# An eight-layer graph and feed-forward network on one core: order of the last expert stage, halves in the top-k search, single tiles in a norm, an earlier bias load

## The chip, the cores and the metric

One core of a Trainium2 chip runs the whole program, one launch from the inputs in HBM to the output in HBM. The metric is the device time of that launch in microseconds, the median of several runs.

## What is computed

Eight layers work one after another on 1250 rows (nodes, or tokens) of 512 numbers, each adding its result to the rows: a graph convolution, a mixture of experts, two graph attention layers with a dense expert layer between them, a feed-forward layer with weights merged from task vectors, a neighbour mean with a layer norm, and a last mixture of experts. Cut to the layers that the change touches:

```python
# L2_gnn: attention, h = x @ W1, then masked softmax over the neighbours, with bias b1, later b2
# L2_ffn: W1m, W2m merged from 8 task vectors
h   = relu(x @ W1m.T + b1m)
out = h @ W2m.T + b2m
y   = layernorm(x + out) * lng + lnb
# L3_ffn: NUM_EXPERTS = 32, GROUP_SIZE = 4, D_FF = 1365, k = 1250 // 32 = 39
Sm = softmax(x @ W_router + b_router)
G, idx = top_k(Sm.T, 39)                        # each expert takes its 39 best tokens
up  = einsum('gjkh,ghf->gjkf', x[idx], W_up)    # one up matrix for each group of 4 experts
act = silu(up + b_up)
E   = einsum('ekf,efh->ekh', act, W_down) + b_down   # one down matrix for each expert
y   = zeros.at[idx].add(G[..., None] * E)
```

## The kernel before, in words

All data are float32. Rows are held as ten tiles of 125 rows by 512. Each layer is a stage (`Stage`) with its own buffers, and at its end all engines meet at a barrier. Inside a stage every engine has its own program, written out by hand, and engines wait for each other by semaphores only; the order of the calls in `sp_program`, `pe_program`, `act_program`, `dve_program` and `pool_program` is the order of the work. SP issues the plain loads and stores in one queue, in order, and GpSimd (POOL) issues indirect gathers and scatters, and some plain copies.

**`gnn2`, the attention stage.** At its start `sp_program` (L2004) issues the mask, the weights, then the two bias vectors (L2008) and further loads. TensorE turns the ten normed tiles, waits for the biases, turns them (L2194), waits until VectorE has copied them (L2362), and then makes the attention rows (`pe_rows`, L2086). ScalarE copies these rows (L2279), and a store and loads through HBM spread them for VectorE's masked maxima (`dve_max`), which need the mask, while TensorE makes the linear products (`pe_linear`, L2114), which need the weights.

**`ffn2`, the merged stage.** At its end TensorE adds up ten tiles of the result in eight PSUM banks. VectorE works by groups of 4, 4 and 2 tiles: `dve_group` takes statistics of each tile (L2575), then mean and variance, and the reciprocal of the root that ScalarE takes; ScalarE normalises each tile out of PSUM (L2524); `dve_finish` multiplies by the merged gain (L2589), adds to the rows (L2591) and takes the statistics for the next layer (L122, `tile_statistics`). The next group's statistics stand ahead of a group's finish.

**`last_layers`, the last two layers.** First products, neighbour sums and the layer norm, tile by tile (`dve_tile`, L2791 on), with router logits. Then `Router.dve_softmax`, and `dve_slots` with `pe_slots` choose the tokens: TensorE turns the ten tiles of weights into 32 rows of 1250, VectorE copies them out of PSUM (L733) and five times finds the eight largest (MAX8, L737), their places (FIND_INDEX8, L738) and blanks them (MATCH_REPLACE8, L741; four times). That makes 40 slots, of which the last has its weight set to 0. The lists are turned and copied to `sw` and `si` (L749, L750).

Then eight groups of four experts. Per group i: POOL gathers 4 x 40 token rows (`pool_gather`), TensorE turns them (`pe_tokens`), VectorE copies them to `xgT` (`dve_tokens`), TensorE makes the up products of all four experts in 11 parts of the inner dimension (`pe_up`, 88 matmul records), ScalarE applies SiLU into the one buffer `hT` (L2929), TensorE makes the down products in two pairs of experts (`pe_down`, 44 records a pair), VectorE multiplies by the weights (`dve_rows`, L2987), and POOL scatters with addition to the output (`pool_scatter`, L2846), each scatter waiting for the one before it. The program order on TensorE is up(i), tokens(i+1), down(i) with both pairs. Up matrices (2.8 MB each) have two buffers, down matrices (2.8 MB each) a ring of five. `sp_program` loads into a buffer as soon as its last reader is done: up matrix i+2 waits for the end of up(i), down matrix e for the pair that used e-5. The last two down matrices are loaded in three parts each, in turn.

## Time and profile before

| | |
|---|---|
| median of 3 runs | 2931.55 us (2931.22 to 2933.32) |
| profiled execution, its own time | 2929.89 us |
| its span in the trace | 2928.1 us |
| mean granted TensorE clock | 0.908 of full |
| busy: TensorE, VectorE, ScalarE, GpSimd | 84%, 55%, 29%, 20% of the span |
| stage `gnn2` begins, `ffn2` begins | 1528, 2253 us |
| `last_layers` begins, tokens chosen, span ends | 2377, 2592, 2928 us |

Times of rows are microseconds from the start of the span. PE is TensorE's matmul side, PEld its weight loads, DVE is VectorE, ACT ScalarE, POOL GpSimd, and SPq the issuing of DMAs by SP. L2846 is a line of the kernel. A granted clock of 1.00 is TensorE at 2.4 GHz, 0.50 at 1.2 GHz. A DMA share of 1 means that all 16 DMA engines are busy.

### The profile page before, as it was taken

The numbers are of one execution on the slowest core, as the hardware profiler recorded it, in microseconds if no ns is written. First come the engines' busy times: TensorE is split into PE (matmuls) and PEld (weight loads), VectorE is DVE, ScalarE is ACT, GpSimd is POOL, SyncE is SP. The second block draws the span as 40 slices with busy tenths as digits, with TensorE's granted clock in tenths as the row PEclk, the third lists the DMA queues.
The fourth block names the chain that finished last, engine by engine and source line by source line (L and its number), as shares of the span: only waits on it lengthen the run. The fifth ranks groups of instructions, "written<-read, shape, count | busy, mean of one in ns | idle before, by whom it ended". The sixth has DMA issues, their size and how long they took to land. (4 is left out here: it accounts for less than half of the span.)

```text
span 2928.1 us, 31276 instructions
## 1 busy us (share of the span) xinstructions
PE 2461.4 (84%) x10766; PEld 1562.6 (53%) x10766; DVE 1624.7 (55%) x3768; ACT 837.2 (29%) x1860; POOL 585.8 (20%) x563
## 2 busy tenths in 40 slices
PE   3899947999957999985568899999999869958877
PEld 1355446999944777774443455344554434434443
DVE  9999353132424889986246898627963354431100
ACT  0155011111112776771111465105641110101110
POOL 0000065455303555420110000000000101012211
PEclk9899957999977999996789999999999989979988
DMA  4000363776724555543443553214541331459996
GB/s 135 0 1 27 120 187 100 260 230 217 260 73 131 155 156 155 152 88 128 125 137 121 194 193 106 89 62 138 189 132 54 127 138 46 144 195 337 347 347 222
DMA packets 195434, 440.43 MB, mean 150 GB/s; under 512 B 25179, under 2 KB 45387, under 8 KB 194798
## 3 DMA queue, kind: packets, MB, share of 16 engines
q1 hardware_dynamic: 156958, 344.67, 35.1%
q0 software_dynamic: 38320, 93.76, 12.3%
q8 instruction: 88, 1.44, 0.2%
q14 instruction: 68, 0.56, 0.1%
HBM read 394.21 MB, written 43.93 MB: 150 GB/s over the span
## 5 line engine op out<-in xcount | busy, mean ns | idle before, releaser
L2124 PE MATMUL psum<-x_res,HH 125*128 125x512 f32 (+1 forms) x960 | 351.7, 525 | 20.2 <-DVE x_res L2314 20.2
L2124 PEld LDWEIGHTS psum<-x_res,HH 125*128 125x128 f32 x960 | 181.3, 193 | 179.8 <-issue 156.4
L1101 POOL DMA_INDIRECT recd<-edge_records,edge_slots x160 | 193.1, 1207 | 293.8 <-issue 287.2
L1468 POOL DMA_INDIRECT hg<-HT,srcidx x196 | 191.2, 975 | 258.5 <-PE psum L1589 128.6
L1630 ACT ACTIVATE hg<-hg,ex 128x129 f32<-128x129 f32 x784 | 235.2, 389 | 1.6
L1589 PE MATMUL psum<-hg,Dh 128*125 128x258 f32 x784 | 208.0, 424 | 6.8 <-DVE ACC L1531 4.3
L2114 PE MATMUL psum<-W,XO 128*125 128x512 f32 x480 | 209.0, 596 | 0.0
L2891 PE MATMUL psum<-wd,XN 128*40 128x512 f32 (+1 forms) x550 | 162.3, 621 | 31.6 <-DMA wd<-in_L_ffn_b_down 22.2
L1589 PEld LDWEIGHTS psum<-hg,Dh 128*125 128x125 f32 x784 | 160.1, 209 | 40.7 <-issue 6.8
L1135 PE MATMUL psum<-xgT,w 128*128 128x187 f32 x1024 | 172.8, 329 | 4.1 <-DMA w<-in_L_ffn_w 4.1
L1135 PEld LDWEIGHTS psum<-xgT,w 128*128 128x128 f32 x1024 | 166.2, 194 | 8.7 <-DMA w<-in_L_ffn_w 5.8
L1144 PE MATMUL psum<-sums_room,w 128*128 128x187 f32 x1024 | 166.1, 322 | 0.0
L1144 PEld LDWEIGHTS psum<-sums_room,w 128*128 128x128 f32 x1024 | 162.9, 190 | 0.0
L2307 DVE SCALAR_TENSOR_TENSOR x_res<-rows,ASD,x_res 125x1250 f32<-125x1250 f32 x80 | 120.7, 1511 | 71.8 <-ACT x_res L2228 71.8
L2114 PEld LDWEIGHTS psum<-W,XO 128*125 128x125 f32 x480 | 90.1, 189 | 115.0 <-issue 114.9
L1208 ACT ACTIVATE sums_room<-psum,b1T 128x187 f32<-128x187 f32 x128 | 53.3, 417 | 282.6 <-PE psum L1135 282.5
L2228 ACT ACTIVATE x_res<-rows,AS 125x1250 f32<-125x1250 f32 x80 | 106.5, 1334 | 95.6 <-PE psum L2124 93.8
L2987 DVE TENSOR_SCALAR x_res<-psum,slot_w 40x512 f32<-40x512 f32 x32 | 23.9, 747 | 195.2 <-PE psum L2891 194.7
L1499 DVE CUSTOM_DVE_ANT_0 junk<-mb,psum 125x512 f32<-125x512 bf16 x196 | 123.1, 684 | 7.8 <-issue 0.9
L2294 DVE CUSTOM_DVE_ANT_0 junk<-MK,rows 125x1250 bf16<-125x1250 bf16 x80 | 116.9, 1461 | 16.4 <-DMA rows<-ROWS 12.4
L2314 DVE SCALAR_TENSOR_TENSOR x_res<-x_res,MK 125x1250 f32<-125x1250 f32 x80 | 116.3, 1454 | 5.4 <-DMA MK<-CT 4.6
L389 PE MATMUL psum<-Sh,Dh 128*125 128x512 bf16 (+1 forms) x588 | 116.4, 347 | 1.8 <-ACT H L596 0.7
(520 smaller groups left out, 3977.0 us busy)
## 6 DMA issues: line engine op xcount, KB each, us to landing
w<-in_L_ffn_w SPq DMA_DIRECT2D x64, 1024.0 KB, 15.1
wd<-in_L_ffn_W_down SPq DMA_DIRECT2D x24, 2560.0 KB
MK<-CT SPq DMA_DIRECT2D x80, 625.0 KB, 3.8
wu<-in_L_ffn_W_up SPq DMA_DIRECT2D x8, 2730.0 KB, 16.4
wd_ahead<-in_L_ffn_W_down SPq DMA_DIRECT2D x6, 2560.0 KB
rows<-ROWS POOLq DMA_DIRECT2D x24, 625.0 KB, 7.2
w<-in_L_ffn_W SPq DMA_DIRECT2D x18, 512.0 KB
t<-in_L_ffn_tv_W SPq DMA_DIRECT2D x16, 512.0 KB
```

The costliest lines, as they stand in the source:

```text
L1101: pool.indirect_dma_start(out=g.recd, out_offset=bass.IndirectOffsetOnAxis(ap=g.posi[:, c:c + 1], axis=0), in_=g.E8[:, c, :], in_offset=No ...
L1135: ins = pe.matmul(g.PS[:, m, 0:CAP], W1[k][:, c, m * 128:(m + 1) * 128], xgT[e % 2][:, c, 0:CAP], start=(c == 0), stop=(c == KC - 1))
L1144: ins = pe.matmul(g.PS[:, 4 + 2 * (e % 2) + c // 2, (c % 2) * SL:(c % 2) * SL + CAP], W2[k][:, m, c * 128:(c + 1) * 128], hT[k % 2][:, m, ...
L1468: pool.indirect_dma_start(out=hg[j % RING][:, c, :], out_offset=None, in_=g.HT, in_offset=bass.IndirectOffsetOnAxis(ap=g.srcidx[:, j * CH ...
L1499: dve.tensor_tensor_reduce(junk[:, h, :], mb[:], bank(h), 1.0, NEG, ALU.add, ALU.max, qm[:, h:h + 1]).then_inc(*top.up())
L1589: ins = pe.matmul(bank(6 + w)[:, 0:HW // 2], Dh[j % 3][:, c, :], hg[j % RING][:, c, w * (HW // 2):(w + 1) * (HW // 2)], start=(c == 0), st ...
L1630: ins = act.activation(heads[:, h, :], heads[:, h, :], ACT.Copy, scale=ex[j % 2][:, c, h:h + 1])
L2114: ins = pe.matmul(PS[0:TP, 2 + i % 3, :], XO[:, c, t * TP:(t + 1) * TP], Wt[:, c, w * 512:(w + 1) * 512], start=(c == 0), stop=(c == kc(l) ...
L2124: return pe.matmul(flat[:, at:at + x1 - x0], HH[:, k, h * DH + c * 128:h * DH + c * 128 + 128], z[n % 4][:, x0:x1], start=(k == 0 and i < ...
L2294: dve.tensor_tensor_reduce(junk[:], MK[0:TP, t, :], RR[h][0:TP, :], 1.0, NEG, ALU.add, ALU.max, MX[:, h, t:t + 1]).then_inc(*head_max.up())
L2307: dve.scalar_tensor_tensor(z[n % 4], RR[2 * (h % 2)][0:TP, :], ASD[:, k, h:h + 1], z[n % 4], ALU.add, ALU.max).then_inc(*mx.up())
L2891: ins = pe.matmul(g.PS[place[k], 4 + k, :], hT[0:deep[m], m, k * SL:(k + 1) * SL], WDn[ring(GS * i + k)][0:deep[m], m, :], start=(m == 0), ...
```

## The change

Four edits.

1. **Last expert stage.** TensorE's order becomes: up(0), tokens(1), and then for each group down pair 0, up(i+1), tokens(i+2), down pair 1. `hT` is held twice, so ScalarE may write group i+1's while group i's is read. SP's order: after the first pair of down loads of a group stands the up load i+3, which waits for up(i+1). The second-to-last down matrix is issued before the wait for the last pair's buffer. POOL gathers three groups ahead and puts a gather between the scatters of a group. 39 token rows in place of 40.
2. **Shorter search.** The turned weights lie as 64 rows of 625 (two halves of the tokens for each expert). Five rounds find 40 of each half; the second half's list is reversed in its first 39 places, and both lists are merged with one comparison by place: the larger of v0[j] and v1[38-j].
3. **Single tiles.** In `ffn2` groups are gone: VectorE handles a tile from its statistics to its sum, ScalarE takes only the root.
4. **Early biases.** In `gnn2` the bias loads stand first in SP's queue.

The diff, cut to its core:

```diff
     def slots(self, count, keep, WT=None, choice=None):
+        self.at = [2 * (t % (NT // 2)) + t // (NT // 2) for t in range(NT)]
+        self.WT = WT if WT is not None else s.sb("weights_by_expert", [2 * ne, N // 2])[:]
...
     def pe_slots(self):
-        for t in range(NT):
-            ins = pe.transpose(g.PS[0:ne, t // 4, (t % 4) * TP:(t % 4 + 1) * TP], self.L[:, t, :],
-                               g.ident[0:TP, 0:TP])
+        for j in range(NT // 2):
+            ins = pe.transpose(g.PS[0:2 * ne, j // 4, (j % 4) * TP:(j % 4 + 1) * TP],
+                               self.L[:, 2 * j:2 * j + 2, :].rearrange("p a e -> p (a e)"), g.ident[0:TP, 0:TP])
...
+        for k, (first, second) in enumerate(((self.val, self.rval), (self.idf, self.rid))):
+            pe.transpose(g.PS[0:self.count, k, 0:ne], first[0:ne, :], g.ident[0:ne, 0:ne])
+            ins = pe.transpose(g.PS[0:self.count, 2 + k, 0:ne], second[ne:2 * ne, :],
+                               g.ident[ne:2 * ne, ne:2 * ne])
...
     def dve_slots(self):
+        dve.tensor_copy(WT[:, 0:4 * TP], g.PS[0:2 * ne, 0, 0:4 * TP]).then_inc(*v.up())
+        dve.tensor_copy(WT[:, 4 * TP:5 * TP], g.PS[0:2 * ne, 1, 0:TP]).then_inc(*v.up())
...
+        dve.tensor_copy(self.rval[ne:2 * ne, 0:n], val[ne:2 * ne, n - 1::-1]).then_inc(*v.up())
+        dve.tensor_copy(self.rval[ne:2 * ne, n:], val[ne:2 * ne, n:]).then_inc(*v.up())
         step(dve.tensor_copy(idf[:], ix[:]))
-        step(dve.tensor_scalar(val[:], val[:], 0.0, None, ALU.max))
-        if self.kept < self.count:
-            step(dve.memset(val[:, self.kept:self.count], 0.0))
+        dve.tensor_scalar(self.rid[ne:2 * ne, 0:n], idf[ne:2 * ne, n - 1::-1], float(N // 2), None,
+                          ALU.add).then_inc(*v.up())
+        dve.tensor_scalar(self.rid[ne:2 * ne, n:], idf[ne:2 * ne, n:], float(N // 2), None, ALU.add).then_inc(*v.up())
...
+        dve.tensor_copy(self.sw[:], v1).then_inc(*v.up())
+        step(dve.tensor_copy(self.diff, t1))
+        dve.tensor_tensor(self.ge, v0, self.sw[:], ALU.is_ge).then_inc(*v.up())
+        step(dve.tensor_tensor(self.diff, t0, self.diff, ALU.subtract))
+        dve.tensor_tensor(self.sw[:], v0, self.sw[:], ALU.max).then_inc(*v.up())
+        step(dve.tensor_tensor(self.diff, self.diff, self.ge, ALU.mult))
+        dve.tensor_tensor(self.si[:], t1, self.diff, ALU.add).then_inc(*v.up())
...
         def sp_program():
+            for l, b in enumerate((b1, b2)):
+                sp.dma_start(br[l * C8:(l + 1) * C8, :], b.rearrange("(c p) -> c p", p=128)).then_inc(*b_in.up(16))
             sp_mask(0)
             sp.dma_start(Wt[:, 0:KC, :], rows_of(W1)).then_inc(*w_in.up(16))
-            for l, b in enumerate((b1, b2)):
-                sp.dma_start(br[l * C8:(l + 1) * C8, :], b.rearrange("(c p) -> c p", p=128)).then_inc(*b_in.up(16))
...
+        def dve_tile(t):
             step = Chain(dve, v)
+            one, res = slice(t, t + 1), g.PS[0:TP, t % 8, :]
+            dve.wait_ge(*down.at(t + 1))
+            step(dve.bn_stats(st[:, t, :], res))
+            step(dve.bn_aggr(mv[:, t, :], st[:, t, :]))
+            dve.tensor_scalar(rs[:, one], mv[:, t, 1:2], EPS, None, ALU.add).then_inc(*var.up())
+            dve.scalar_tensor_tensor(XN[0:TP, t, :], res, mv[:, t, 0:1], lng[:], ALU.subtract,
+                                     ALU.mult).then_inc(*normed.up())
+            dve.wait_ge(*root.at(t + 1))
+            dve.reciprocal(rs[:, one], rs[:, one]).then_inc(*ready.up())
+            dve.wait_ge(*normed.now())
+            dve.wait_ge(*ready.now())
+            step(dve.scalar_tensor_tensor(g.X[:, t, :], XN[0:TP, t, :], rs[:, one], g.X[:, t, :], ALU.mult, ALU.add))
+            tile_statistics(g, t)
...
-    SG = GS * SL
+    SG = GS * K
...
             sp_down(NR - 2, 0, FM, lw[ring(NR - 2)])
+            sp.wait_ge(*mu.at(FM))
+            sp_up(2)
             for i in range(NG - 1):
-                if i + 2 < NG:
-                    sp.wait_ge(*mu.at(FM * (i + 1)))
-                    sp_up(i + 2)
                 for e in range(GS * i + NR, GS * i + NR + GS):
                     if e < NE:
                         sp.wait_ge(*md.at((e - NR) // 2 + 1))
                     if e < NE - 2:
                         sp_down(e, 0, FM, lw[ring(e)])
+                    elif e == NE - 2:
+                        for j, (m0, m1) in enumerate(PARTS):
+                            sp_down(e, m0, m1, last_pair[j])
+                    if e == GS * i + NR + 1 and i + 3 < NG:
+                        sp.wait_ge(*mu.at(FM * (i + 2)))
+                        sp_up(i + 3)
             for j, (m0, m1) in enumerate(PARTS):
-                for e in (NE - 2, NE - 1):
-                    sp_down(e, m0, m1, last_pair[j])
+                sp_down(NE - 1, m0, m1, last_pair[j])
...
             for i in range(NG):
-                if i + 2 < NG:
-                    pool_gather(i + 2)
                 for k in range(GS):
+                    if k == GS // 2 and i + 3 < NG:
+                        pool_gather(i + 3)
                     pool_scatter(GS * i + k)
...
             pe_tokens(0)
+            pe_up(0)
+            pe_tokens(1)
             for i in range(NG):
-                pe_up(i)
+                pe_down(i, 0)
                 if i + 1 < NG:
-                    pe_tokens(i + 1)
-                pe_down(i)
+                    pe_up(i + 1)
+                if i + 2 < NG:
+                    pe_tokens(i + 2)
+                pe_down(i, 1)
...
             for i in range(NG):
-                if i:
-                    act.wait_ge(*md.at(GS // 2 * i))
+                if i >= 2:
+                    act.wait_ge(*md.at(GS // 2 * (i - 1)))
...
             for i in range(NG):
-                if i == 0:
-                    dve_tokens(0)
-                if i + 1 < NG:
-                    dve_tokens(i + 1)
-                dve_rows(i)
+                dve_rows(i, 0)
+                if i + 2 < NG:
+                    dve_tokens(i + 2)
+                dve_rows(i, 1)
```

## Rows read from the trace of the kernel before

**Rows 1.** Stretches, last stage: us; busy of each engine; PEclk, DMA share, GB/s.

```profile
2585.00:2616.00 31.00, 16.21 (x106) 15.66 (x106) 7.18 (x13) 5.52 (x12) 7.52 (x8) 0.67 0.08 22
...
2650.00:2700.00 50.00, 42.18 (x241) 21.15 (x239) 6.13 (x8) 4.33 (x11) 16.23 (x14) 0.97 1.05 334
...
2902.00:2928.00 26.00, 12.83 (x60) 3.42 (x56) 2.99 (x4) 0.00 (x0) 5.72 (x4) 0.83 0.12 17
```

**Rows 2.** Timeline, TensorE: start, us, instruction, idle before and its releaser.

```profile
2831.14 11.05 PE L2891 MATMUL psum<-wd,XN 128*40 128x512 f32 x44 [7.45 <-DMA wd<-in_L_ffn_b_down]
```

**Rows 3.** Timeline of SP's queue, last stage.

```profile
2615.68 0.39 SPq L2691 DMA_DIRECT2D wu<-in_L_ffn_W_up  x1
2626.99 0.39 SPq L2695 DMA_DIRECT2D wd_ahead<-in_L_ffn_W_down  x1
```

**Rows 4.** Chain of waits, near its end: start, us, what.

```profile
2872.02 11.10 PE psum L2891 x44
2883.11 12.16 PE psum L2869 x88
...
2895.74 19.11 PE psum L2891 x88
```

**Rows 5.** Timeline of POOL, last stage, the scatters.

```profile
2884.19 1.43 POOL L2846 DMA_INDIRECT out<-x_res,slot_i  x1 [8.62 <-DVE x_res L2987]
2892.57 1.43 POOL L2846 DMA_INDIRECT out<-x_res,slot_i  x1 [6.94 <-DMA out<-x_res,slot_i]
...
2915.92 1.43 POOL L2846 DMA_INDIRECT out<-x_res,slot_i  x1 [3.47 <-DVE x_res L2987]
2920.29 1.43 POOL L2846 DMA_INDIRECT out<-x_res,slot_i  x1 [2.94 <-DMA out<-x_res,slot_i]
```

**Rows 6.** Timeline, TensorE, start of the attention stage.

```profile
1546.32 0.28 PE L2194 MATMUL psum<-ident,bias_rows 16*128 16x16 f32 x1 [7.03 <-DMA bias_rows<-in_L_gnn_b]
1546.87 10.41 PE L2086 MATMUL psum<-XO,att 128*8 128x512 f32 x24 [0.27 <-DVE biases L2362]
```

**Rows 7.** Stretches at the start of the attention stage, columns as rows 1.

```profile
1537.00:1541.00 4.00, 2.11 (x15) 1.32 (x13) 1.19 (x3) 2.49 (x5) 0.00 (x0) 1.00 1.04 410
...
1545.00:1550.00 5.00, 3.42 (x5) 0.68 (x6) 0.17 (x1) 0.00 (x0) 0.00 (x0) 0.50 1.03 388
```

**Rows 8.** POOL's plain stores of normed tiles (tensor XND), issue to landing.

```profile
DMA to landing us min/median/max: 2.7/2.7/8.6
```

**Rows 9.** Timeline, VectorE, end of the merged stage.

```profile
2333.99 0.70 DVE L2575 BATCH_NORM_STATS2 st<-psum 125x6 f32<-125x512 f32 x1 [5.59 <-PE psum L2500]
2336.50 0.70 DVE L2575 BATCH_NORM_STATS2 st<-psum 125x6 f32<-125x512 f32 x1 [1.80 <-PE psum L2500]
...
2362.05 1.28 DVE L2575 BATCH_NORM_STATS2 st<-psum 125x6 f32<-125x512 f32 x2
...
2376.03 0.69 DVE L122 BATCH_NORM_STATS2 ln_st<-x_res 125x6 f32<-125x512 f32 x1
```

**Rows 10.** Timeline, VectorE, one tile of `last_layers`' `dve_tile`: both statistics.

```profile
2543.55 0.69 DVE L2798 BATCH_NORM_STATS2 st<-wd 125x6 f32<-125x512 f32 x1
...
2546.33 0.69 DVE L2809 BATCH_NORM_STATS2 ln_st<-x_res 125x6 f32<-125x512 f32 x1
```

**Rows 11.** Groups by form, VectorE, search: count, busy us, mean ns, idle before.

```profile
L737 DVE MAX8 slot_value<-records 32x8 f32<-32x1250 f32 x5 | 7.3, 1451 | 0.2
L738 DVE FIND_INDEX8 top_index<-slot_value,records 32x8 uint32<-32x1250 f32 x5 | 7.2, 1442 | 0.0
L741 DVE MATCH_REPLACE8 records<-slot_value,records 32x1250 f32<-32x1250 f32 x4 | 5.7, 1432 | 0.0
L733 DVE COPY records<-psum 32x500 f32<-32x500 f32 x2 | 1.3, 662 | 2.4 <-PE psum L716 2.4
L733 DVE COPY records<-psum 32x250 f32<-32x250 f32 x1 | 0.4, 397 | 0.0
```

**Rows 12.** Timeline, VectorE, a small operation behind the search.

```profile
2590.62 0.17 DVE L742 CAST slot_token<-top_index 32x40 f32<-32x40 uint32 x1
```

More of the change, by code:

```diff
@@ L645, in __init__ @@
         self.v = s.sig("dve_steps")
+        self.at = list(range(NT))
         self.loaded, self.out = s.sig("router_loaded"), s.sig("logits_out")
@@ L2415, in ffn2 @@
         norm = Norm(g, s, XT=XT, XN=XN)
-        groups = ((0, 4), (4, 8), (8, NT))
         def sp_program():
@@ L2518, in act_program @@
                                    bias=b1c[:, f:f + 1]).then_inc(*relu.up())
-            for i, (t0, t1) in enumerate(groups):
-                act.wait_ge(*var.at(i + 1))
-                act.activation(rs[:, t0:t1], rs[:, t0:t1], ACT.Sqrt).then_inc(*root.up())
-                act.wait_ge(*ready.at(i + 1))
-                for t in range(t0, t1):
-                    act.activation(XN[0:TP, t, :], g.PS[0:TP, t % 8, :], ACT.Identity, bias=nb[:, t:t + 1],
-                                   scale=rs[:, t:t + 1]).then_inc(*normed.up())
+            for t in range(NT):
+                act.wait_ge(*var.at(t + 1))
+                act.activation(rs[:, t:t + 1], rs[:, t:t + 1], ACT.Sqrt).then_inc(*root.up())
         def pool_program():
@@ L2601, in dve_program @@
             dve.wait_ge(*lnb_in.at(1))
-            dve_group(0, *groups[0])
-            for i in range(len(groups)):
-                if i + 1 < len(groups):
-                    dve_group(i + 1, *groups[i + 1])
-                dve_finish(i, *groups[i])
+            for t in range(NT):
+                dve_tile(t)
         sp_program()
@@ L2657, in last_layers @@
         first = Norm(g, s, xn=[XN[:, u, :] for u in range(2)], xT=xT[0])
-        place = [slice(64 * (k % 2), 64 * (k % 2) + SL) for k in range(GS)]
+        place = [slice(64 * (k % 2), 64 * (k % 2) + K) for k in range(GS)]
         free = WU[1][:].rearrange("p a b -> p (a b)")[:, NT * D:]
@@ L2667, in last_layers @@
                            view(spare, TP, nw, NT, NE)))
-        rt.slots(SL, K, old[0:NE, 0:N])
+        rt.slots(SL, K, old[0:2 * NE, 0:N // 2], [g.iota_tp[0:SL, k * NE:(k + 1) * NE] for k in range(2)])
         norm = rt.norm
-        xg, xgT = XN[0:SL, 0:GS, :], view(XN_all[:, 2 * GS:, :].rearrange("p a d -> p (a d)"), 128, 0, KC, SG)
-        hT = XN_all[:, GS:2 * GS, :].rearrange("p a d -> p (a d)")[:, 0:FM * SG].rearrange("p (m n) -> p m n", m=FM)
-        wo = g.X[0:SL, 0:2 * GS, :]
+        xg, end = XN[0:K, 0:GS, :], XN_all[:, 2 * GS:, :].rearrange("p a d -> p (a d)")
+        xgT = view(end, 128, 0, KC, SG)
+        half = view(XN_all[:, GS:2 * GS, :].rearrange("p a d -> p (a d)"), 128, 0, FM, SG)
+        hT = [[half[:, m, :] for m in range(FM)], [old[:, m * SG:(m + 1) * SG] for m in range(FM - 1)] +
+              [end[:, KC * SG:(KC + 1) * SG]]]
+        wo = g.X[0:K, 0:2 * GS, :]
         listed, gathered = s.sig("slots_listed"), s.sig("gathered0")
@@ L2978, in dve_tokens, with dve_rows @@
                             g.PS[:, 0:2, 0:2 * SG]).then_inc(*tc.up())
-        def dve_rows(i):
-            for k in range(GS):
+        def dve_rows(i, pair):
+            for k in (2 * pair, 2 * pair + 1):
                 e = GS * i + k
                 row = wo[:, e % (2 * GS), :]
-                dve.wait_ge(*md.at(GS // 2 * i + k // 2 + 1))
+                dve.wait_ge(*md.at(GS // 2 * i + pair + 1))
                 if e >= 2 * GS:
                     dve.wait_ge(*scattered.at(16 * (e - 2 * GS + 1)))
-                dve.tensor_scalar(row, g.PS[place[k], 4 + k, :], rt.sw[:, 0, e:e + 1], None,
+                dve.tensor_scalar(row, g.PS[place[k], 4 + k, :], rt.sw[0:K, e:e + 1], None,
                                   ALU.mult).then_inc(*ev.up())
```

115 lines of the change are left out of this document (43 added, 72 removed).

## The prediction

> **What bounds the kernel now.** The profile was read in this order: busy time over stretches of the last stage, the chain of waits, the timeline of each queue, and then the two places further up that the change touches. The kernel runs its stages one behind the other with a barrier between, so microseconds saved in one stage are saved at the end, if nothing in that stage takes them back.
>
> In the last stage the reader is to see two regimes [rows 1]. From 2585 to 2616 the DMA engines stand almost still (share 0.08, 22 GB/s): tokens are chosen, gathered and multiplied by the first up matrix, and no further weights may be loaded until that product frees its buffer. From 2650 on the share is 1.05, and after 2902 it is 0.12. TensorE waits for down weights there, 7.45 us before one pair [rows 2]. So from about 2616 to 2902 this stage is a fixed amount of bytes at a fixed rate. Reordering TensorE can't shorten it. What counts is when the stream may start, whether it ever runs dry, and what is left once it has ended. The start is the load of the third up matrix at 2615.68, which waits for the end of the first up products; the next load waits for the first down pair at 2626.99 [rows 3]. The rest is the chain at the end: a pair of downs at 2872.02 as soon as its weights land, up products 12.16, both last pairs 19.11 [rows 4], then the scatters, of which each waits for the one before [rows 5].
>
> **Early biases (attention stage).** The bias rows are issued behind the mask and the weights, and TensorE takes them only at 1546.32 after 7.03 us without work; the attention products follow at 1546.87 and take 10.41 [rows 6]. Two small transfers at the head of the queue should land well before the transposes ahead of them in TensorE's order end, at 1546.32 - 7.03 = 1539.3. Then the products start 1546.87 - 1539.9 = 6.9 earlier. There is more: the granted clock was 1.00 (2.4 GHz) from 1537 to 1541, behind the transposes, and 0.50 (1.2 GHz) from 1545 to 1550, behind the idle time [rows 7]. The products ran at half speed until a little after 1550, about 3.5 us, half of which, 1.8, goes too: together 8.7. Against it: the products' row is then stored while the DMA engines are still full (share 1.03 until 1550 [rows 7]). Stores on this queue landed in 2.7 us when quiet, at most 8.6 [rows 8]. I take 1 us of that, as the engines empty within a microsecond or two of that store: **-7.7**, bounds -5.8 and -8.8. Mask and weights move back by under 1 us and are used later than 1551, which costs nothing. VectorE's chain and TensorE's product chain of the stage both begin behind this point, so the gain stays.
>
> **Single tiles (merged stage).** Before, VectorE starts its first statistics at 2333.99 and starts its last at 2376.03, ending at 2376.72 [rows 9]; TensorE delivers a tile each 2.5 to 2.6 us, and VectorE waits for whole groups, then works them off. The new tile is the sequence which the last stage already has: from its first statistics to the second 2.78 us [rows 10], plus 0.6 until the next may start (two statistics in a row take 1.28, one 0.70 [rows 9]) = 3.38. Ten make 33.8, more than TensorE's 26, so VectorE alone decides: 2333.99 + 33.8 + 0.1 = 2367.9, **-8.8**. The 2.78 hold ScalarE's root already. Bounds -8.2 (0.05 more on each tile) and -9.0.
> The Trainium skill ("VectorE: DVE Perf Modes", section on the TRN2 errata) says that each VectorE instruction pays a fixed latency, that many small tiles pay it per tile, and that one should tile to 512 elements or more, which speaks against this edit; by its fixed term of some 150 cycles, thirty tiny operations in place of nineteen cost 1.7 us more, which would leave 7.1 if they were not in the 2.78 already.
>
> **Shorter search.** Five rounds on 1250 elements: five times 1451, five times 1442, four times 1432 ns [rows 11]. The copies there take 662 ns for 500 elements and 397 for 250: 1.06 ns per element, so 625 fewer save 0.66 on each of 14 instructions, 9.3. No row shows 64 partitions for 32, but row lengths, not partitions, set the price everywhere here. Five transposes for ten save 1.1 of their 2.3; copying 625 columns for 1250 saves 0.7. Added: two more small operations ahead of the last transposes, two more transposes, and seven for two operations behind them, in four dependent steps; small ones cost 0.17 [rows 12]. That is 0.3 + 0.15 + 0.87. Copies with a reversed order are in no row: at best they cost like the others, at worst 0.3 more each. Net 9.3 + 1.1 + 0.7 - 1.3 = **-9.8**, bounds -9.0 and -10.3. This shifts the gathers, the first up products and the restart of the stream one for one; weights for the first groups land before 2585 [rows 1].
>
> **Order of the last stage.** Loads, their bytes and their wait for the first up products stay. 39 columns for 40 save at most a fortieth of 12.16, 0.3, of the first up products; taken as nothing. The stream must not dry up: the fourth up matrix now waits for the second up products, at 2626.99 + 12.2 = 2639.2, while two down matrices (33 matrices in the 286 us from 2616 to 2902: 8.7 each) are under way until 2644.4; the next two down matrices wait for the second pair, 1.7 + 9.6 later, 2650.5, while the up matrix runs until 2653. It holds, by 2 to 3 us. So the stream ends as before, less the shift. The down matrix after the wait in [rows 4] and its three followers keep their places; two places earlier (8.2 us each, from 2831.14 to 2872.02 for five [rows 2, 4]) its predecessor lands at 2855.6. TensorE: first pair of the seventh group 2855.6 + 10.6 (between 9.6 and the 11.1 after a wait) = 2866.2, last up products +12.2 = 2878.4, then three pairs of 9.6 and 0.6 of waiting: 2907.8 instead of 2914.85, **-7.0 on TensorE**. But scatters take 8.4 us each under load (2884.19 to 2892.57) and 4.4 when quiet [rows 5]. Experts 26 and 27 are ready at 2888.8 (before: 2884): 2889.8, 2898.2, 2904.7, 2909.1, 2913.5, the last at 2917.9 instead of 2920.29. The chain of scatters, not TensorE, sets the end. That is -2.4; as 8.4 is one interval and they may be quicker, I take **-2.8**, with 0 and -7.4 as bounds.
> A scatter now has 39 rows for 40. By the Trainium skill ("DMA: Bandwidth & Descriptors", section "Why a DMA increments its semaphore by 16 and not by 1") a transfer is spread over the largest number of engines up to 16 that divides its rows, 10 for 40 and 13 for 39; if that held for these, the loaded scatters would be a quarter shorter and the term nearer -5.
>
> **Sum.** 7.7 + 8.8 + 9.8 + 2.8 = 29.1. The profiled execution took 2929.9 (span 2928.1), so 2900.8; the median of the runs is 2931.55, 1.7 above it, and the forecast stands on that: **2902.5**. All least gains, with 1 us of a dry stream, give 22 less; all largest 36.5 less: 2909.6 and 2895.1.
>
> **Rivals.**
> (a) The tail follows TensorE. For it: the scatters of the pairs before may be quicker than 8.4. Then the last term is 7: 2898.3. Chance 0.18.
> (b) The biases gain nothing: another load or store takes their place, or VectorE's masks decide. Against it: both chains of the stage start behind these products. 2910.2. Chance 0.07.
> (c) The stream runs dry, and the kernel is slower. SP's queue is in order: the up load that waits for the next group's up products holds back the two down loads behind it. If the matrices under way were used up in that time, each of five or six groups would stand idle for up to 12.2 us of up products; with 5 groups 61 us: 2963.5. It decides as soon as the loads queued ahead last less than the 22 us of a pair and the up products; in steady flow six loads, some 50 us, stand ahead, so only the start (2 to 3 us of margin) is near. Chance 0.03.
> (d) The search is not shortened: the doubled partitions cost double. 2912.3. Chance 0.04.
> The forecast has 0.64, and 0.04 is left for what I overlook. A measurement can tell 0.2% here, 5.9 us. All but (c) are faster by more; half of the rest goes to faster and half to no change: 0.95 faster, 0.02 same, 0.03 slower. The range, 2895 to 2911, holds the forecast's bounds, (a) and (b).
>
> **What would show it.** Right: TensorE doesn't idle ahead of the bias transpose; the merged stage ends some 34 us after its first statistics; eight-element searches near 0.79 us; the third up matrix loaded 26.3 us earlier than now; share 1.05 without a dip until about 2876; the last scatters 4.4 apart without waiting for VectorE. Wrong: a dip of the DMA share in the first 40 us of the stream, pairs of 39 rows that scatter slower, or a search that keeps its 21 us.

## Result and the profile after

The changed kernel takes **2893.56 us** (median of 4 runs, 2890.28 to 2897.89) against 2932.44 for the kernel before beside it: ratio 0.9872, 95% interval 0.9859 to 0.9886, so 38.9 us less. The forecast was 2902.5 us with a range of 2895 to 2911; the sign is right, and the gain was 1.4 us larger than even the range allowed. The profiled execution took 2891.68 us, its span is 2889.7 us at a mean granted clock of 0.916.

Stretches of the last stage in the changed kernel (us; busy of PE, PEld, DVE, ACT, POOL; PEclk, DMA share, GB/s):

```profile
2555.00:2585.00 30.00, 15.04 (x104) 14.77 (x105) 7.71 (x24) 5.00 (x11) 7.41 (x8) 0.66 0.38 134
2616.00:2666.00 50.00, 49.43 (x285) 25.51 (x282) 6.78 (x9) 5.45 (x14) 12.28 (x10) 1.00 1.05 350
2867.00:2889.00 22.00, 8.57 (x40) 2.73 (x36) 1.50 (x2) 0.00 (x0) 5.61 (x4) 0.78 0.14 21
```

They answer to [rows 1]: the same three regimes, but from 30 to 80 us into the stream it carries 350 GB/s, where from 34 to 84 us it had 334 before, at the same share of 1.05. These windows flatter the change: over the whole stream it is 343 GB/s against 338. TensorE's clock is 1.00 in this stretch (0.97 before).

SP's queue, as [rows 3]:

```profile
2585.75 0.39 SPq L2686 DMA_DIRECT2D wu<-in_L_ffn_W_up  x1
2597.06 0.39 SPq L2690 DMA_DIRECT2D wd_ahead<-in_L_ffn_W_down  x1
...
2608.91 0.39 SPq L2686 DMA_DIRECT2D wu<-in_L_ffn_W_up  x1
```

The third up load starts at 2585.75 instead of 2615.68, the next down load 11.3 us later as before, and the fourth up load now 23.2 us behind the third instead of 37.4.

The chain of waits at the end, as [rows 4] (start, us, what):

```profile
2844.76 9.78 DMA wd<-in_L_ffn_b_down
2854.53 0.14 issue
2854.67 9.66 PE psum L2889 x44
...
2865.12 0.76 DVE x_res L2991
2865.89 0.04 issue
2865.92 9.66 PE psum L2889 x44
...
2877.80 3.39 DMA out<-x_res,slot_i
```

and POOL's last scatters, as [rows 5]:

```profile
2855.08 1.41 POOL L2845 DMA_INDIRECT out<-x_res,slot_i  x1 [12.92 <-DVE x_res L2991]
2863.03 1.40 POOL L2845 DMA_INDIRECT out<-x_res,slot_i  x1 [6.54 <-DMA out<-x_res,slot_i]
2869.54 1.41 POOL L2845 DMA_INDIRECT out<-x_res,slot_i  x1 [5.11 <-DMA out<-x_res,slot_i]
2873.69 1.40 POOL L2845 DMA_INDIRECT out<-x_res,slot_i  x1 [2.74 <-DMA out<-x_res,slot_i]
2877.80 1.41 POOL L2845 DMA_INDIRECT out<-x_res,slot_i  x1 [2.71 <-DVE x_res L2991]
2881.98 1.40 POOL L2845 DMA_INDIRECT out<-x_res,slot_i  x1 [2.78 <-DMA out<-x_res,slot_i]
```

with VectorE's rows of the last pair:

```profile
2875.61 1.53 DVE L2991 TENSOR_SCALAR x_res<-psum,slot_w 39x512 f32<-39x512 f32 x2 [9.73 <-PE psum L2889]
```

Of the last six scatters the profile gives four to the landing of the one before, and those of 2855.08 and 2877.80 to VectorE. The second of these is doubtful. The first of VectorE's two rows was done after half of 1.53 us, at 2876.4, and before the change the scatter followed 1.04 us behind such a start (2914.88 to 2915.92), which would have been 2876.65 here. It came 4.11 us behind the scatter before it, like its neighbours (4.15 and 4.18), so it too waited for a landing. No up products stand there any more: the last two pairs are separate, with 1.6 us between them for VectorE.

Attention stage, as [rows 6]:

```profile
1537.57 0.23 PE L2202 MATMUL psum<-ident,bias_rows 16*128 16x16 f32 x1
1538.41 8.56 PE L2094 MATMUL psum<-XO,att 128*8 128x512 f32 x24 [0.61 <-ACT XO L201]
```

The same two stretches of that stage as [rows 7]:

```profile
1537.00:1541.00 4.00, 3.39 (x14) 1.25 (x14) 0.17 (x1) 1.16 (x2) 0.00 (x0) 1.00 1.04 412
1545.00:1550.00 5.00, 3.71 (x18) 1.83 (x17) 0.41 (x2) 1.20 (x1) 0.58 (x1) 1.00 0.99 366
```

TensorE has no idle time ahead of the bias rows, the clock stays at 1.00 (2.4 GHz), and the products take 8.56 us instead of 10.41, 1.85 less.

Merged stage, VectorE, two successive tiles, as [rows 9]:

```profile
2326.95 0.68 DVE L2578 BATCH_NORM_STATS2 st<-psum 125x6 f32<-125x512 f32 x1
...
2329.66 0.69 DVE L122 BATCH_NORM_STATS2 ln_st<-x_res 125x6 f32<-125x512 f32 x1
2330.27 0.68 DVE L2578 BATCH_NORM_STATS2 st<-psum 125x6 f32<-125x512 f32 x1
```

A tile takes 3.32 us. The search, groups by form (count, busy us, mean ns), as [rows 11]:

```profile
L737 DVE MAX8 half_value<-records 64x8 f32<-64x625 f32 x5 | 4.0, 804 | 0.2
L738 DVE FIND_INDEX8 top_index<-half_value,records 64x8 uint32<-64x625 f32 x5 | 4.0, 795 | 0.0
L741 DVE MATCH_REPLACE8 records<-half_value,records 64x625 f32<-64x625 f32 x4 | 3.1, 786 | 0.0
...
L742 DVE COPY turned_value<-half_value 32x39 f32<-32x39 f32 x1 | 0.2, 173 | 0.0
```

An instruction on 64 rows of 625 takes 647 ns less than one on 32 rows of 1250, close to the 663 that 625 elements cost at the 1.06 ns of the copies in [rows 11]; the doubled partitions add nothing that can be seen. The copy in reversed order (L742) takes 173 ns, a straight operation of that size 0.17 us [rows 12].

**Where the 38 us are.** The stretches below are cut at issues of SP's queue (the attention stage's first load, its first load of counts, the merged stage's first load, the last stage's first and third up load) and at the end of the weight stream, which is where the DMA share falls for good. That end is read in windows of 2 us, so the last two rows are good to about 1 us.

| us in the profiled runs | before | after | difference | forecast |
|---|---|---|---|---|
| up to the attention stage | 1528.5 | 1527.1 | -1.4 | 0 |
| attention stage to its counts (biases) | 101.3 | 94.5 | -6.8 | -7.7 |
| from there to the merged stage (same code) | 623.4 | 620.4 | -3.0 | 0 |
| merged stage to first up load (tiles) | 143.8 | 135.4 | -8.4 | -8.8 |
| first to third up load (search) | 218.7 | 208.4 | -10.3 | -9.8 |
| weight stream | 285.7 | 280.9 | -4.8 | 0 |
| tail behind the stream | 26.7 | 23.0 | -3.7 | -2.8 |

Three upstream terms came as forecast (25.5 against 26.3). What was missed is the weight stream, 4.8 us shorter, and 4.4 us in stretches that run the same code in both kernels.

### The profile page after: what moved, and what is told of

It is laid out like the page before. It is cut to its first block and busy times, and to the rows that moved or that the text cites. A ratio compares the mean times of both kernels' runs of the same rounds, so it can differ in the third digit from the quotient of the medians.

```text
span 2889.7 us, 31294 instructions
## 1 busy us (share of the span) xinstructions
PE 2447.9 (85%) x10763; PEld 1555.9 (54%) x10763; DVE 1617.5 (56%) x3786; ACT 831.9 (29%) x1857; POOL 587.2 (20%) x563
## 5 line engine op out<-in xcount | busy, mean ns | idle before, releaser
L1109 POOL DMA_INDIRECT recd<-edge_records,edge_slots x160 | 194.5, 1216 | 292.4 <-issue 285.7
L2991 DVE TENSOR_SCALAR x_res<-psum,slot_w 39x512 f32<-39x512 f32 x32 | 23.9, 747 | 187.8 <-PE psum L2889 187.3
L2302 DVE CUSTOM_DVE_ANT_0 junk<-MK,rows 125x1250 bf16<-125x1250 bf16 x80 | 116.9, 1461 | 17.9 <-DMA rows<-ROWS 13.8
L2268 ACT ACTIVATE x_res<-x_res 125x1250 f32<-125x1250 f32 x80 | 99.0, 1237 | 30.6 <-DVE x_res L2315 29.6
```

Source lines behind the costliest of these rows:

```text
L1109: pool.indirect_dma_start(out=g.recd, out_offset=bass.IndirectOffsetOnAxis(ap=g.posi[:, c:c + 1], axis=0), in_=g.E8[:, c, :], in_offset=No ...
L2302: dve.tensor_tensor_reduce(junk[:], MK[0:TP, t, :], RR[h][0:TP, :], 1.0, NEG, ALU.add, ALU.max, MX[:, h, t:t + 1]).then_inc(*head_max.up())
```

## Experiments

Each group of four ran on one chip, beside the kernel before, whose median was 2961.0 us for t1 to t4, 2964.6 for t5 to t8, 2931.2 for t9 to t12 and 2935.0 (one run) for t13 to t16. Medians are compared within a group only. Stretches of the trace are compared over all. "Stream" is the time from the third up load to the end of the weight stream; in the five traces with the old order and 40 rows its length was 284.9 to 285.7.

**t1: the changed kernel again**, with no edit.

> The changed kernel once more, as the yardstick of the next three. Measured before: 2893.6 us, and from the load of the third up matrix to the end of the weight stream 280.3 us, against 286.3 in the kernel before; the prediction had taken this as unchanged. If that was chance of one profiled execution (drift), this one's stream lies anywhere between 280 and 286. If it belongs to the change, it is 280 +- 1 again, and the time 2893.6 +- 2.

Measured 2924.4 us, ratio 0.9887 (0.9870 to 0.9904), 36.6 us less than before. Stream 281.3, third up load to the end of the span 304.4 (first trace 304.0; before 312.4). The shorter stream belongs to the change. Drift is ruled out for it: the six traces of the new order with all transfers and with the last two matrices loaded as in the change (the first one, t1, t3, t7, t9, t10) have 280 to 281.6.

**t2: old order, 39 rows.** On all queues the order of before, for instance on TensorE:

```diff
-            pe_up(0)
-            pe_tokens(1)
             for i in range(NG):
-                pe_down(i, 0)
+                pe_up(i)
                 if i + 1 < NG:
-                    pe_up(i + 1)
-                if i + 2 < NG:
-                    pe_tokens(i + 2)
-                pe_down(i, 1)
+                    pe_tokens(i + 1)
+                for pair in range(GS // 2):
+                    pe_down(i, pair)
```

> The changed kernel with the old order of the last stage on all queues (both down pairs together, up load i+2 ahead of the down loads, two gathers ahead, the last two matrices interleaved), but 39 rows. Theory 'rows' (39 rows for 40 in gathers and scatters shorten the stream): stream 280, only the tail's 2.4 us are lost, 2896. Theory 'order' (the new order keeps the stream fuller): stream 286, tail 26, 2902. Theory 'drift': stream anywhere, 2896.

**t3: new order, 40 rows**, the same in places, transposes, weights and scatters; the last parts of the second `hT` lie elsewhere to make room.

```diff
-    SG = GS * K
+    SG = GS * SL
...
-        xg, end = XN[0:K, 0:GS, :], XN_all[:, 2 * GS:, :].rearrange("p a d -> p (a d)")
+        xg, end = XN[0:SL, 0:GS, :], XN_all[:, 2 * GS:, :].rearrange("p a d -> p (a d)")
```

> The changed kernel with its new order but 40 rows an expert in gathers, products and scatters (the 40th keeps the weight that the merge gives it, so each expert adds one token more than the reference). Theory 'rows': stream 286, 2893.6 + 6 + 0.3 for the first up products = 2900. Theory 'order': stream 280, 2894. Theory 'drift': 2894, stream anywhere.

**t4: both undone** (the edits of t2 and t3).

> Both undone: old order and 40 rows in the last stage, with the shorter search, the single tiles and the early biases kept (the 40th row keeps its weight here too). Stream 286 and tail 26 by 'rows' and by 'order': 2902. 'Drift': 2896. Beside the kernel before (2932.4) this is what the three upstream edits are worth: 26.3 by the prediction, so 2905 to 2906 if nothing else was gained there; 29 to 30 by the traces of before and after.

| | median, us | ratio to before | stream | up load 3 to end |
|---|---|---|---|---|
| t1 new order, 39 | 2924.4 | 0.9887 (0.9870 to 0.9904) | 281.3 | 304.4 |
| t2 old order, 39 | 2931.0 | 0.9893 (0.9874 to 0.9911) | 284.0 | 311.1 |
| t3 new order, 40 | 2926.4 | 0.9892 (0.9876 to 0.9908) | 281.6 | 305.6 |
| t4 old order, 40 | 2936.8 | 0.9923 (0.9909 to 0.9936) | 285.6 | 312.6 |

t4 is within 0.2 us of the kernel before in both stretches (285.7 and 312.4), so nothing else in the last stage plays a part. The order gives 6.7 us with 39 rows (311.1 to 304.4) and 7.0 with 40 by the traces, 6.7 and 10.4 by the medians. The rows give 1.2 to 1.5 by the traces, nearly all of it in the stream in the old order (1.6) and in the tail in the new one. So "order" holds for most of the time from the third up load to the end, and "rows" for a little; neither theory had this split of the stream. The ratios' intervals overlap between t1, t2 and t3; t4 alone stands clear of t1. Its 24.2 us are the three upstream edits together: 26.3 had been forecast.

**t5: 39 rows in transfers, 40 in products, old order.**

```diff
-            pool.indirect_dma_start(out=xg[:, k, :], out_offset=None, in_=g.XND,
-                                        in_offset=bass.IndirectOffsetOnAxis(ap=rt.si[0:SL, e:e + 1], axis=0)
+            pool.indirect_dma_start(out=xg[0:K, k, :], out_offset=None, in_=g.XND,
+                                        in_offset=bass.IndirectOffsetOnAxis(ap=rt.si[0:K, e:e + 1], axis=0)
```

> Old order of the last stage, upstream edits kept, gathers and scatters of 39 rows as in the change, but transposes and products over 40 columns (the 40th row is a stale one and is not scattered). With the old order the stream took 286.1 us with 40 rows (as in the kernel before) and 284.3 with 39. Theory 'transfers' (smaller gathers and scatters leave the weight stream more of the engines): 284.3. Theory 'TensorE' (shorter products free the buffers earlier and so keep more loads under way): 286. The dip of the DMA share some 265 us into the stream is there in both. Tail 26 to 27.

Stream 282.0, third up load to the end 309.2; 2934.1 us, ratio 0.9893 (0.9876 to 0.9909). "Transfers" holds, "TensorE" falls: what 39 rows give in the stream comes from smaller gathers and scatters. The stream is even 2.0 us shorter than t2's, of which a smaller dip of the DMA share (below) makes 1.1; the rest is not explained.

**t6: the last two matrices loaded as before.**

```diff
-                    elif e == NE - 2:
-                        for j, (m0, m1) in enumerate(PARTS):
-                            sp_down(e, m0, m1, last_pair[j])
...
-                sp_down(NE - 1, m0, m1, last_pair[j])
+                for e in (NE - 2, NE - 1):
+                    sp_down(e, m0, m1, last_pair[j])
```

> The changed kernel, but matrices 30 and 31 are loaded in turn, both only after the wait for the last pair's buffer, as before. Theory 'dip' (of the new order's gain one part is that matrix 30 no longer waits, so the DMA engines don't fall idle some 265 us into the stream): the dip comes back, the stream is 1.5 to 2.5 us longer than the changed kernel's 281.5, so 283 to 284, and the end moves by as much. Theory 'products in between alone': no dip, because the pair ahead of it ends earlier now; stream 281.5, time unchanged.

The stream took 286.0 us and fell nearly silent 262 to 270 us into it. These two stretches are of t6 (columns as above):

```profile
2894.00:2898.00 4.00, 4.00 (x22) 1.10 (x18) 0.00 (x0) 0.00 (x0) 0.00 (x0) 1.00 0.40 136
2898.00:2902.00 4.00, 4.00 (x20) 1.09 (x18) 1.47 (x2) 0.00 (x0) 0.46 (x1) 1.00 0.06 18
```

and these, of t4 and of the kernel before, lie at nearly the same place in their streams:

```profile
2882.00:2886.00 4.00, 4.00 (x26) 2.72 (x23) 1.50 (x2) 0.39 (x1) 1.30 (x1) 1.00 0.75 253
...
2881.00:2885.00 4.00, 4.00 (x24) 2.37 (x21) 1.50 (x2) 0.39 (x1) 0.81 (x1) 1.00 0.74 265
```

t1 has 1.06 and 1.05 in the same place (2875 to 2883). The dip is shown, and larger than either theory had it. In t6 SP has issued matrix 29 by 2890.88, 258.4 us into the stream, and waits 9.7 us for the buffer of the last pair (to 2900.56). Before the change it came to that wait 5.3 us later, at 2879.33, and waited 3.9 us. But the end moved by 0.6 us only (305.0 against 304.4), not with the stream: "and the end moves by as much" was wrong. t6's chain of waits from 2901.54 on is scatters alone, with three of them taking 7.04, 6.23 and 4.19 us:

```profile
2901.54 7.04 DMA out<-x_res,slot_i
...
2909.38 6.23 DMA out<-x_res,slot_i
...
2916.41 4.19 DMA out<-x_res,slot_i
...
2921.40 3.40 DMA out<-x_res,slot_i
```

**t7: last up products before the pair that waits.**

```diff
             for i in range(NG):
+                if i == NG - 2:
+                    pe_up(NG - 1)
                 pe_down(i, 0)
-                if i + 1 < NG:
+                if i + 1 < NG - 1:
                     pe_up(i + 1)
```

> The changed kernel with the last group's up products ahead of the seventh group's first down pair, where TensorE had waited 6.3 us for down weights. Theory 'TensorE sets the tail' (behind that wait it ran without a pause but two of 0.8 and 1.7 us until 2903.8 of a span of 2917.6): the wait is filled, the last product ends some 3 us after the last weights land, and the end comes 4 to 6 us earlier: tail 17 to 19 us instead of 22.6. Theory 'scatters set the tail' (my prediction: each waits for the one before it, 4.1 us apart): TensorE ends earlier, the scatters keep their times, tail 22 to 22.6. Weights and gathers are as in the changed kernel, stream 281.5.

Third up load to the end 303.4, 1.0 less than t1; 2932.2 us, ratio 0.9892 (0.9876 to 0.9909), no difference from t1. Both theories' numbers missed, as TensorE did not end earlier. The pair behind the moved products ended later, so the load of matrix 29, which waits for it, was issued at 2877.33 and landed at 2895.29; TensorE idled 7.2 us for it, its clock fell to 0.50, and it ended at 2916.9, 290.4 us into the stream (t1: 290.6):

```profile
2894.00:2898.00 4.00, 2.57 (x7) 0.71 (x9) 0.00 (x0) 0.00 (x0) 1.19 (x1) 0.50 1.06 361
```

**t8: biases alone.** The hunk in `gnn2`'s `sp_program`, nothing else.

> The kernel before with the early biases alone. By my prediction 7.7 us less (5.8 to 8.8), all of it between the attention stage's first issue and its first load of counts: 101.3 before, 93.6 here (five traces with the whole change or its upstream edits: 93.6 to 94.7), with a granted clock of 1.00 in the products. Rival 'the later part of that stage gains too' (in the first pair of traces another 3.0 us went between there and the merged stage): 10.7 less. On the other chip that stretch scattered between 622 and 625 us with the same code, so I expect no more than 7.7.

2959.2 us, ratio 0.9982 (0.9972 to 0.9991), 5.5 us less; the stretch took 93.9 instead of 101.3, with the products at 8.56 us as in the changed kernel. From there to the merged stage 623.5 (before 623.4): the rival falls, and the 3.0 us of the first pair of traces do not belong to the edit. Over fourteen traces this stretch of unchanged code lay between 620.4 and 626.8.

**t9: the last up products cut in two.**

```diff
+                if i == NG - 2:
+                    pe_up(NG - 1, 0, 6)
                 pe_down(i, 0)
                 if i + 1 < NG:
-                    pe_up(i + 1)
+                    pe_up(i + 1, 6 if i == NG - 2 else 0)
```

> The changed kernel, with the last group's up products cut in two: parts 0 to 5 ahead of the seventh group's first down pair, in the 6 us in which TensorE waits for its weights, and the rest between its two pairs, as before. Moving them whole (t7) had delayed that first pair and with it the load of matrix 29, so that TensorE idled 7.2 us later. Theory 'scatters set the tail': the second pair is done some 6 us earlier, its two scatters start earlier, and the chain gains 2 us until the last two pairs, which now wait for weights: from the third up load to the end 302 to 302.5 us against 304.4 (t1) and 304.0. Theory 'TensorE sets the tail': weights of matrix 29 land only some 269 us into the stream, then two pairs of 9.7: no more than 1.4 us gained, 303.

303.4 us from the third up load to the end, 1.0 less than t1; 2897.5 us, ratio 0.9884 (0.9867 to 0.9900). This is the size that "TensorE sets the tail" gave (no more than 1.4), and its chain shows why: TensorE waits until 2860.03 for matrix 29, and then both pairs follow.

```profile
2849.97 10.05 DMA wd<-in_L_ffn_b_down
2860.03 0.14 issue
2860.16 21.43 PE psum L2889 x88
```

VectorE's rows of the last pair, and POOL's scatters around them, show that here TensorE sets the end by way of VectorE. The scatter after VectorE's start follows it by 1.04 us and its predecessor by 5.08, where a chain of landings has 4.1 to 4.2:

```profile
2881.62 1.52 DVE L2993 TENSOR_SCALAR x_res<-psum,slot_w 39x512 f32<-39x512 f32 x2 [7.92 <-PE psum L2889]
...
2877.58 1.40 POOL L2845 DMA_INDIRECT out<-x_res,slot_i  x1 [2.96 <-DMA out<-x_res,slot_i]
2882.66 1.41 POOL L2845 DMA_INDIRECT out<-x_res,slot_i  x1 [3.68 <-DVE x_res L2993]
```

**t10: matrix 29 in three parts as well.**

```diff
+                    elif e == NE - 3:
+                        for j, (m0, m1) in enumerate(PARTS):
+                            sp_down(e, m0, m1, in_parts[j])
```

> As t9, and matrix 29 is loaded in three parts too, each with a semaphore of its own, so that the pair 28, 29 may start before its last part has landed. TensorE's last product then ends some 3 us after the last weights (285 into the stream instead of 290.6). If the scatters bind, the chain from matrix 24's rows on sets the end: 300 to 301 us from the third up load to the end, 4 us less than t1; if they did not, 298.

304.7 us in the trace, 2896.2 us, ratio 0.9876 (0.9860 to 0.9893): no gain over t1. The first part of matrix 31, issued at 2860.30, landed at 2872.55, when the stream was at its end; the pair could not start before it and took 11.52 us behind that wait:

```profile
2860.30 12.25 DMA wd<-in_L_ffn_W_down
2872.55 0.14 issue
2872.69 11.52 PE psum L2897 x44
```

My expectation that the last product ends 3 us after the last weights was wrong: a part that is issued into a full queue lands with what stands ahead of it, 12 us later here.

**t11: search alone, t12: tiles alone** (their hunks of the change; t11 has the old order and 40 rows).

> The kernel before with the shorter search alone; last stage in the old order with 40 rows (the 40th keeps the weight that the merge gives it). Prediction 9.8 us less (9.0 to 10.3). The five traces which hold the search took 208.4 to 210.9 us from the last stage's first to its third up load, against 218.7 without, so I expect 9.0 now; rival 'the upstream edits overlap in what they save': 7 or less alone.

> The kernel before with the single tiles alone. Prediction 8.8 us less (8.2 to 9.0), all of it between the merged stage's first issue and the last stage's first up load: 143.8 us before, 133.6 to 135.4 in the five traces that hold the edit, so 134.5 to 135.

t11 took 2921.5 us, ratio 0.9967 (0.9950 to 0.9983), 9.7 us less; its stretch fell from 218.7 to 209.4. t12 took 2922.1 us, ratio 0.9972 (0.9963 to 0.9982), 9.1 us less; its stretch fell from 143.8 to 134.9. In company the same stretches gave 7.7 to 10.3 (search) and 8.4 to 10.4 (tiles) in fourteen traces. By the medians the parts add up to 5.5 + 9.7 + 9.1 = 24.3, and t4 had 24.2, so no overlap shows; an agreement to 0.1 is luck, as each median is good to a few us only.

**t13 to t16: streams without scatters, and without gathers.** t13 and t15 are t4's kernel, t14 and t16 the changed one. In the first two no scatter of the last stage is made, in the other two also no gather but the first group's. The edit of t13:

```diff
-            pool.indirect_dma_start(out=out, out_offset=bass.IndirectOffsetOnAxis(
-                ap=rt.si[0:SL, e:e + 1], axis=0), in_=wo[:, e % (2 * GS), :], in_offset=None,
-                compute_op=ALU.add).then_inc(*scattered.up(16))
+            pool.nop().then_inc(*scattered.up(16))
```

> The kernel of t4 (old order, 40 rows, upstream edits kept) without any scatter of the last stage: the experts' rows are weighted but not added to the output. Read is the stream from the third up load to the end of the weights: 286.1 with scatters. Their 2.2 MB in that time cost 6.4 us at 343 GB/s, so 279.5 if a scattered byte costs what a weight byte does, less if more. Theory 'how the scatters fall': old order and new order differ only by the dip, 1 to 2 us, once scatters are gone. Theory 'order of the loads': they still differ by 4.5 to 5.

> The changed kernel (new order, 39 rows) without any scatter of the last stage. Stream with scatters 281.3 to 281.8; without 275 by their bytes. 'How the scatters fall': 278 to 279, since t13 falls further than this one. 'Order of the loads': 275 or less, 4.5 to 5 below t13.

> t13 without the gathers of groups 1 to 7 as well (all groups compute on the first group's tokens): weights alone are moved. 92.3 MB at 343 GB/s are 269 us. If neither scatters nor gathers make the difference of the orders, t15 and t16 differ as t4 and t1 do, by 4.5; if gathers make it, by the dip alone.

> t14 without the gathers of groups 1 to 7: weights alone in the new order. 'How the small transfers fall': equal to t15 but for the dip, 1 to 2 us shorter. 'Order of the loads' (whether down and up matrices stand in the queue together): 4.5 shorter.

| stream, us | old order, 40 rows | new order, 39 rows | difference |
|---|---|---|---|
| all transfers (t4, t1) | 285.6 | 281.3 | 4.3 |
| no scatters (t13, t14) | 277.3 | 273.6 | 3.7 |
| no scatters, no gathers (t15, t16) | 266.0 | 267.0 | -1.0 |

"Order of the loads" falls: with weights alone the new order is no shorter. The scatters cost about the same in both, 8.3 and 7.7 us. The gathers cost 11.3 in the old order with 40 rows and 6.6 in the new one with 39, and that is the difference. The expectation that scatters make it was wrong, the one for the gathers right. By their bytes (2.0 MB in this time, at 343 GB/s) gathers would cost 5.7. Each of these runs was executed once, so a length is good to about 1 us. Order and rows change together from column to column, so they don't say which of the two makes gathers cheaper, and why it does isn't settled.

The streams of the old order hold a dip of the DMA share, also where the small transfers are gone, only earlier. The first of these stretches is of t13, the second of t15:

```profile
2854.19:2856.19 2.00, 2.00 (x15) 1.82 (x14) 1.50 (x2) 0.37 (x1) 0.00 (x0) 1.00 0.59 124
...
2840.53:2842.53 2.00, 2.00 (x12) 0.93 (x9) 0.68 (x1) 0.00 (x0) 0.00 (x0) 1.00 0.54 183
```

Over its windows t13 falls short of a share of 1 by 1.6 us and t15 by 1.7, so the 11.3 of the gathers are not made by it; less the dip, weights alone take 264.3 in the old order against 267.0 in the new one. Less what the share fell short of 1 in the dip (1.1 us before, 2.6 in t2, 1.5 in t5), the streams are 284.6 before, 281.4 in t2, 280.5 in t5, 281.3 in t1 and 281.6 in t3: either 39 rows or the new order takes the 3.3 us away, and both together take no more.

In t16 the share also falls to 0.77, between 36 and 38 us after the third up load, which it does in no run of this order with gathers: the forecast's margin against a dry start is as thin as it said.

t14 shows what scatters do to the tail. Without them the changed kernel's last product ended 283.7 us into the stream and the span 5.4 later, at 289.1, against 304.4 for t1.

## Why the prediction was right and wrong

**Biases, right.** -7.7 was forecast with bounds of 5.8 and 8.8; the trace of the change has -6.8, the edit alone -7.4 and -5.5 by its medians. The medians lie just under the lower bound, with an interval of 2.7 to 8.3 us. Both halves are there: the products start 7.1 us earlier within the stage (6.9 forecast), and at a clock of 1.00 they take 1.85 us less (1.8 forecast). What was taken too small is the loss behind them: 2.1 us in the trace of the change, where 1 was allowed for the store.

**Tiles, right.** -8.8 was forecast; -8.4 in the change, -8.9 and -9.1 alone. A tile took 3.32 us instead of the 3.38 read from the last stage, which is 0.6 on ten tiles. The Trainium skill ("VectorE: DVE Perf Modes", section on the TRN2 errata) warns of a fixed latency for each instruction; by an estimate from its figure 7.1 would have been left if the rows of the last stage did not hold that latency already. The gain has been above that in every trace with the edit (8.4 to 10.4): the tiny operations cost no more than those rows had them at.

**Search, right.** -9.8 was forecast; -10.3 in the change's first trace, -9.2 by the trace and -9.7 by the medians alone, but less than 9.0, the lower bound, in most of the traces with several edits; where that last microsecond goes is not traced. Its 14 large instructions gave 9.1 of the 9.3 counted on: 5 x 647, 5 x 647 and 4 x 646 ns. Row length sets the price here, and the doubled partitions don't show in it: 804 ns for 64 rows of 625 against 1451 for 32 of 1250.

**The stream, wrong.** The step that failed is "So the stream ends as before, less the shift." I had read it as a fixed amount of bytes at a fixed rate, and it came 4.8 us shorter (4.3 by t4 against t1). Two things break that. The old order had a dip where SP waited for the last pair's buffer with both last matrices still to load. It makes 1.1 us, and the windows I read (2650 to 2700, and from 2902 on) did not show it; one at 2881 to 2885 has a share of 0.74. The rest comes from the small transfers beside the weights, which I had not priced at all. With weights alone the new order is no shorter (267.0 against 266.0). Gathers cost 11.3 us in the old order with 40 rows and 6.6 in the new one with 39, where their bytes come to 5.7. So much is shown; why they cost more in the one than in the other stays open. My reason against a dry stream held: no dip in the first 40 us but the one at 10 to 13 us, which is in both kernels, though t16 shows how near it was.

**The tail, right in its mechanism, and its size 0.9 us too small.** -2.8 was forecast, and -3.7 came (-3.9 by t4 against t1: 27.0 and 23.1). "The chain of scatters, not TensorE, sets the end" holds for the changed kernel, but by 1 us only. In the kernel before and in all others of the old order that keep their scatters TensorE sets it: the span ends 12.9 to 13.3 us behind the last product. So it does in t7, t9 and t10 (13.0 to 13.1). In the changed kernel it is 14.1 us (t1 13.8, t3 15.0, t6 15.4), since the last scatters are still waiting for each other. That is why t7 and t9 gained 1 us against t1 and t10 nothing: with the scatters out of the way TensorE's last product, which did not end earlier (290.4 to 291.6 us into the stream, t1 290.6), takes over. The size was off because scatters are quicker: 4.1 to 4.2 apart where 4.4 was said, and 7.95 under load where 8.4 was.

Rival (a), that the tail follows TensorE to -7, gave 2898.3 and was nearer in time, but by luck. TensorE gained 9.3 us (its last product ended 299.2 us into the stream before, at 2914.85, and 289.8 in the changed kernel, at 2875.58), of which 4.8 are the shorter stream, so its own gain was 4.5 and not 7. And had it set the end, 13.0 us behind its last product, the end would have been 302.8 us into the stream, not 304.0.

By the Trainium skill ("DMA: Bandwidth & Descriptors", section "Why a DMA increments its semaphore by 16 and not by 1") 39 rows would spread over 13 engines and 40 over 10; from that the forecast estimated that loaded scatters would be a quarter shorter. The trace doesn't agree in that size: a loaded one took 7.95 from issue to issue (2855.08 to 2863.03) against 8.38 before, 5% less. That 39 rows are cheaper than 40 by more than their bytes shows in the old order alone.

**What belongs to no step.** 4.4 us of the first pair of traces lie in code that is the same in both (1.4 ahead of the attention stage, 3.0 behind its biases). Such stretches scattered by 6 us over the traces. In the second measurement the change gave 36.6 us, and the sum of what the traces tie to it is 25.5 + 8.5 = 34.0. So of the miss of 9 us, 5.7 are the stream and the tail (4.8 and 0.9), and the rest is inside what one pair of measurements scatters. The range missed because it gave the stream no bound on the side of a gain; with the 36.6 us of the second measurement the time would have been 2895.0, on its edge. There is also a slip in the sum: the largest gains (8.8, 9.0, 10.3 and 7.4) add up to 35.5 us and not 36.5, so that bound should have been 2896.1.

## What to carry to other kernels

A stage that is bound by its weights is not a constant: look through the whole stream in windows of a few microseconds, for dips at waits of the load queue as well as for its rate, and price small transfers that run beside it apart. Where loads, TensorE and a serial chain of scatters end within a microsecond or two of each other, moving one of them earlier gives a microsecond or nothing, because the next one takes over (t7, t9, t10). And halving the row length of a search by using twice the partitions saves almost half its time (45% of each of its large instructions here).

## What was not expected

- 2.0 MB of gathers lengthened the weight stream by 11.3 us in one order with 40 rows and by 6.6 in another with 39, at the same DMA share of 1.05 in the middle of the stream.
- The profile put the wait of a scatter down to VectorE, whose row had been done more than a microsecond before; only the distances of 4.1 us between scatters showed that the landing before it was what it waited for.
- Products that fill TensorE's idle time can cost it elsewhere: the pair behind them frees its buffers later, and the load that waits for them is late (t7: 7.2 us of idle time and a clock of 0.50 afterwards).
- A small part of a matrix issued last landed 12.25 us later, with the rest, so that loading in parts bought nothing (t10).
- The same kernel took 2931 to 2935 us on some chips and 2961 to 2965 on others. The weight stream had the same length on both, 285.7 and 284.9 us (before, and t8). The attention stage began at 1528.5 on the one and at 1560.1 on the other (t8), so the difference lay ahead of all that is changed here.
